# A decoder layer on one core: products with the values on 17 columns instead of 68, and the first pair of k projected ahead of q

## The reference

```python
x = x + mamba(layernorm(x))                            # state-space block, chunks of 64 tokens
x = x + cross_attention(layernorm(x), ctx, mask)       # 16 heads of 64
x = x + ffn(layernorm(x))                              # self attention, then experts

# cross_attention: q from x, k and v from the context
scores = q @ k.T + mask ; ctx = softmax(scores) @ v ; return ctx @ Wo.T

# self attention inside ffn: 16 query heads of 16, 4 key heads, causal, rotary
k = repeat(k, 4) ; v = repeat(v, 4)
scores = where(causal, q @ k.T / 4, -inf) ; out = softmax(scores) @ v ; return out @ wo

# experts: top 2 of 4, gated
```

## Time and profile before

| | us |
|---|---|
| median of 3 runs | 1392.12 |
| lowest and highest run | 1389.46, 1392.37 |
| the profiled execution | 1387.37 |
| its span, first to last instruction | 1385.5 |
| TensorE busy | 1252.3 |
| VectorE busy | 941.3 |
| ScalarE busy | 677.8 |
| GpSimd busy | 271.7 |

### The profile page before, as it was taken

The page is one execution under the profiler, slowest core; times in us unless marked ns, Lnnn a source line. Parts: engine busy times, 40 slices in busy tenths (PEclk is TensorE's granted clock), DMA queues, the critical chain, the costliest instruction groups (busy, mean ns, idle before and its releaser), DMA issues. The chain is left out here.

```text
span 1385.5 us, 25269 instructions
## 1 busy us (share of the span) xinstructions
PE 1252.3 (90%) x8404; PEld 1108.9 (80%) x8404; DVE 941.3 (68%) x2935; ACT 677.8 (49%) x1527; POOL 271.7 (20%) x281
## 2 busy tenths in 40 slices
PE   5889998999899898998998989899897479999997
PEld 4668988867799797778988967799797458888886
DVE  6867767777576676756767776577676875555553
ACT  4737627653565474635636654466374413333332
POOL 2001005110000330100005110000250084333332
PEclk9999999999999999999999999999999579999999
DMA  6026400010452001016500010453611012222221
GB/s 250 1 47 144 115 17 1 1 61 1 116 138 53 16 1 62 1 29 152 126 16 1 1 61 1 106 125 75 229 61 34 1 23 39 38 35 38 39 40 23
DMA packets 45661, 80.38 MB, mean 58 GB/s; under 512 B 8448, under 2 KB 18176, under 8 KB 45024
## 3 DMA queue, kind: packets, MB, share of 16 engines
q1 hardware_dynamic: 37376, 69.19, 18.5%
q0 software_dynamic: 6720, 9.18, 4.1%
q10 hardware_dynamic: 1440, 0.39, 0.1%
HBM read 28.01 MB, written 8.78 MB: 27 GB/s over the span
## 5 line engine op out<-in xcount | busy, mean ns | idle before, releaser
L1036 ACT ACTIVATE b_pp<-b_pp,b_nm 128x256 f32<-128x256 f32 x256 | 116.0, 501 | 83.6 <-DVE b_nm L1074 82.7
L912 PEld LDWEIGHTS bank<-b_va,b_pt 128*128 128x128 f32 x1024 | 128.6, 193 | 4.4
L912 PE MATMUL bank<-b_va,b_pt 128*128 128x65 f32 x1024 | 129.2, 270 | 0.0
L1371 PE MATMUL bank<-c_v,c_pt 128*128 128x68 f32 x768 | 102.2, 269 | 4.1 <-DVE c_pt L1597 3.5
L1371 PEld LDWEIGHTS bank<-c_v,c_pt 128*128 128x128 f32 x768 | 97.2, 191 | 7.8 <-DVE c_pt L1597 7.0
L1074 DVE CUSTOM_DVE_ANT_0 b_pp<-bank,mask 128x256 f32<-128x256 f32 x256 | 97.0, 417 | 0.0
L100 PE MATMUL bank<-e_up_low,e_xh 128*128 x210 | 90.8, 432 | 6.6 <-DVE e_xl L208 5.0
L1899 ACT ACTIVATE e_th<-bank 128x512 f32<-128x512 f32 x35 | 21.0, 601 | 152.8 <-PE bank L102 152.8
L1349 PE MATMUL bank<-c_kv,c_qv 128*128 128x128 f32 (+1 forms) x512 | 89.2, 298 | 0.0
L197 PE MATMUL bank<-identr 128*128 128x512 f32 x274 | 75.6, 426 | 14.9 <-DVE a_cv L617 8.2
L1589 DVE CUSTOM_DVE_ANT_0 c_pp<-bank,const 128x128 f32<-128x128 f32 (+1 forms) x256 | 80.0, 350 | 11.3 <-PE bank L1349 10.8
(11 more groups left out here) (403 smaller groups left out, 3658.2 us busy)
## 6 DMA issues: line engine op xcount, KB each, us to landing
b_kst<-b_kh SPq DMA_DIRECT2D x128, 128.0 KB, 2.3
k_low_twice<-b_kl SPq DMA_DIRECT2D x128, 128.0 KB, 2.4
b_qst<-b_ql SPq DMA_DIRECT2D x64, 128.0 KB, 2.4
raw_up<-in_w SPq DMA_DIRECT2D x4, 768.0 KB, 10.4
raw_down<-in_w SPq DMA_DIRECT2D x4, 768.0 KB, 12.1
XN<-in_x SPq DMA_DIRECT2D x5, 512.0 KB, 3.8
context<-in_ctxT SPq DMA_DIRECT2D x4, 512.0 KB, 5.9
mask<-in_mask SPq DMA_DIRECT2D x4, 512.0 KB, 6.8
```

The costliest lines, as they stand in the source:

```text
L912: ins = pe.matmul(O2[u % 2][:, at:at + VW], pt[:, n % 2, kt * S + qt * P:kt * S + (qt + 1) * P], va[:, b * QT + kt, 2 * j + hp, :], start= ...
L1036: act.activation(pp[:, n % 3, qt, :], pp[:, n % 3, qt, :], ACT.Exp, bias=nm[:, n % 4, qt:qt + 1], scale=-1.0).then_inc(s["probs_exp"], 1)
L1371: ins = pe.matmul(OB[u % 2][:, at:at + AKV * AVW], pt[:, n % 4, i * P:(i + 1) * P], v[:, b * QT + kt].rearrange("p a b -> p (a b)"), start ...
```

## The change

Two edits, independent of each other. In cross attention TensorE's list starts with k0 and v4 and then q0, v5, where it started with v4, v5, q0, k0; ScalarE and VectorE take the results in the new order, and `projected`, which gives the count that ScalarE waits for, is changed to fit. SP's list is the same. In self attention `values` multiplies with the 17 columns of its head's own key head, and `normalise` reads them where they now lie.

```diff
         def projected(j, which):
-            return 2 * j + which + 1 if j < 2 else 2 * j + (1 - which) + 1
+            return 2 * j + which + 1 if j == 1 else 2 * j + (1 - which) + 1
...
             ins.then_inc(s["x_turned"], 1)
+            project(0, 1)
             project_v(4)
-            project_v(5)
             pe.wait_ge(s["x_low"], KD)
             project(0, 0)
-            project(0, 1)
+            project_v(5)
             project_v(6)
             project_v(7)
...
                 part_high(act, uh[:, k, :], T2[k][:]).then_inc(s["x_high"], 1)
+            place(0, 1)
             place_v(1)
             place_v(2)
+            place(0, 0)
             place_v(3)
             place_v(4)
-            place(0, 0)
-            place(0, 1)
             place_v(6)
...
                 part_low(dve, ul[:, k, :], T2[k][:], uh[:, k, :]).then_inc(s["x_low"], 1)
+            place_low(0, 1)
+            place_low(0, 0)
             place_v(5)
-            place_low(0, 0)
-            place_low(0, 1)
             place_v(7)
...
             def values(n):
                 u, hp = n // 2, n % 2
-                b = where(n)[1]
+                m, b, _ = where(n)
...
                 for qt, i, kt in ((0, 0, 0), (1, 1, 0), (1, 2, 1)):
-                    at = (hp * QT + qt) * AKV * AVW
-                    ins = pe.matmul(OB[u % 2][:, at:at + AKV * AVW], pt[:, n % 4, i * P:(i + 1) * P],
-                                    v[:, b * QT + kt].rearrange("p a b -> p (a b)"), start=kt == 0, stop=kt == qt)
+                    at = (hp * QT + qt) * AVW
+                    ins = pe.matmul(OB[u % 2][:, at:at + AVW], pt[:, n % 4, i * P:(i + 1) * P],
+                                    v[:, b * QT + kt, m], start=kt == 0, stop=kt == qt)
...
-                src = OB[u % 2][:, 0:2 * QT * AKV * AVW].rearrange("p (h q d) -> p h q d", h=2, q=QT)
+                src = OB[u % 2][:, 0:2 * QT * AVW].rearrange("p (h q d) -> p h q d", h=2, q=QT)
                 o = rc[:, u % 2].rearrange("p (h q) -> p h q", h=2)
-                ch.link(dve.reciprocal(o, src[:, :, :, m * AVW + AD]))
+                ch.link(dve.reciprocal(o, src[:, :, :, AD]))
...
-                                  src[:, :, :, m * AVW:m * AVW + AD],
+                                  src[:, :, :, 0:AD],
```

## The result

The kernel became slower. The median of four runs is 1436.16 us (1427.26 to 1481.56), beside 1391.12 us for the kernel before (four runs, 1389.46 to 1392.37). The ratio is 1.0313, with an interval of 1.027 to 1.0357; it leaves out the run of 1481.56 us, in which the clock was lowest. The profiled execution took 1427.49 us, its span is 1425.6 us, 40.1 us more than before.

The account below looks back on a forecast made before the run. Cross attention was taken as bound by TensorE, busy 102.98 of 108.10 us, with waits at its start to win. Part one 4 x 2.2 + 2 x 0.15 = 9.1 us, part two 0: from 1392.12 to 1383.0 us, range 1376.5 to 1388.5.

Parts of the forecast that it names:

- Part one, k's first pair first: Start of cross attention: k0 in v4's place removes the 1.8 us wait for q; 9.1 us won over four groups.
- Where the stall goes next: Cross attention: ScalarE's copy of k2 waits 1.7 us for k1's transfers, leaving a shift of 2.2 us a group.
- The clock at this place: Cross-attention start: granted clock falls behind the gaps in two groups, as now; between 2.6 us won and 2.6 lost.
- Part two, 0 for the columns: Self attention: 17 columns for 68 win 0 us, since weight loads about 0.11 us apart set the pace.
- the rival of 18 us: Self attention: TensorE streams fewer columns and they pay, 18 us more won, 1365 us; chance 0.04.
- the estimate of 4.5 us from the Trainium skill's spacing rule: Self-attention products: (30.8 - 25) ns x 768 = 4.5 us won, making the sum 13.6; placed with the 0.04 rival.
- the last rival: Self-attention head-loop pauses: clock falls, 1.3 us each, seven eat the 9.1, ten make it slower; chance 0.11, 0.07 slower.

Follow-up runs that it names:

- the order alone: The changed kernel with `values` and `normalise` as before (68 columns), only the new cross-attention order kept: 1380.35 us, ratio 0.9938 to the kernel before.
- The experiment with k1 early: New order with 68 columns, and k1 and q1 moved ahead of v6 and v7 so k1 is sent earlier: 1371.05 us, ratio 0.986.
- the columns alone: The kernel before with only the 17 columns in self attention, old order kept: four runs of 1437.45, 1463.92, 1497.40 and 1505.48 us.

## Why the prediction was wrong

**Part one, k's first pair first: right, in place and in size.** The sum said 9.1 us; the cross stages lost 8.6, and the order alone won 8.7 us.
- The steps of group 0 came within 0.4 us, and the whole stage began 0.43 us earlier than in the kernel before (GpSimd's setting of the ones at 86.53, before at 86.96), so against the stage's start they came within 0.1: SP's first k transfer at 89.70 (said 90.05), the second issue for q begins by 95.4 (said 95.8), the first scores at 100.05 (100.5), the first masking at 100.72 (101.1). The wait for q is gone.
- "Where the stall goes next" was right: the copy of k2 waits, at 104.48 (104.1), for 2.38 us in group 0 and 1.55 in the others, where 1.7 was said. Against the stage's start that is 0.8 us late in group 0, where one of k1's transfers took 3.1 us to land and not 2.3, and to 0.1 us as said in group 1. In group 3 the second transposes come 2.1 us earlier, measured from the setting of the ones (2.2 said). The experiment with k1 early showed that it is k1's transfers that hold the copy.
- "The clock at this place": two falls of 1.3 us were taken. Before, groups 1 and 2 fell; after, group 0 alone falls, and it takes 3.4 us longer than groups 1 to 3, of which 0.8 are the longer wait for k1's transfers. Without these the stages lost 437.23 - 2.6 - (428.60 - 3.4) = 9.4 us, so the 9.1 holds. That the two falls taken and the one that came cost about the same is luck.

**Part two, 0 for the columns: right at full clock, wrong as an account of what the edit does.** Loads 0.112 us apart with 17 columns, and 1366.59 us beside 1366.06, show that fewer columns win nothing that can be told from the spread; the rival of 18 us and the estimate of 4.5 us from the Trainium skill's spacing rule did not come. But the argument asked only what the columns cost at the clock of the rows. The streamed columns also kept that clock up, at a pause that is in the loop either way.

**Two steps failed, both about the clock in self attention.** The first is the 0 of part two, which took the clock as given ("stages of the same length, clock 1.00"): in the profiled execution the 17 columns cost 51.0 us, in two stages. The second is the price in the last rival, which was there for this case: "Each fall costs 1.3 us, as in group 1". The rival named the right place, the pause of the earlier trace rows, and the right direction; at 1.3 us it took ten falls to be slower. A fall costs 25.8 us, and one is enough, against the 9.1 won. The 1.3 us was read where the products behind the fall are four transposes, six products of 512 columns and eight of 65, and the clock comes back within the stretch of the earlier trace rows. That this would also hold in a loop with 17 columns was never argued; the price was carried over from one kind of work to another. The runs show the difference directly: the loop with 68 columns raised the clock some 6 us after the work began again, in three stages of four, and lost about 3.9 us; the loop with 17 did not raise it in the 53 us that were left of it, and ten wide products raised it.

The chance of 0.11 rested on "the pauses in this loop are short, and no self-attention stage falls now". The clock of 1.00 in the earlier trace rows was read as a property of the pause. It was one of the pause and of the columns around it: pauses of 0.77 to 0.92 us let the clock go in two stages of four with 17 columns, and those of 0.76 to 0.98 us in none with 68.

**What stays open.** In the profiled execution groups 0 and 2 kept their clock at the same pause at which groups 1 and 3 lost it, and in the columns alone groups 2 and 3 fell. The length of the pause does not decide it: groups 0 to 3 waited 0.90, 0.84, 0.77 and 0.92 us in the kernel after, and 0.90, 0.82, 0.76 and 0.91 in the columns alone; and the pause of 1.19 us at the start of the loop lost no clock. No run here tells what does. Nor is it shown what the chip counts; the runs tell only that at 17 columns the clock falls at this pause and stays down to the end of the loop, that at 34 one run of five took as long as two falls would make it, and that at 68 none fell at the short pause.

## What to carry to other kernels

An edit that makes TensorE stream less per weight load can be free in time and still cost the clock: look at every pause in the loop, not only the longest (here 0.84 us lost the clock, and 1.19 us at the start did not), and ask what would raise the clock again behind it. The price of a fall is to be read from work like that which follows it, for it is the time until the clock comes back, and a loop that does not raise it pays to its end. When a start-up stall is removed, follow the serial queue to the next buffer that comes free late; here that gave a second win as large as the first, in part because a fall of the clock behind the stall went with it.

## What was unexpected in the hardware

- TensorE busy in 40.00 of 40.00 us, by the profile, with the granted clock at 0.50 throughout. Being busy without a gap, as the profile counts it, did not raise it.
- A pause of 0.84 us was enough to lose the clock in a loop that had held 1.00 until then, through a pause of 1.19 us too.
- At the low level weight loads follow each other almost twice as slowly, here (527.26 - 525.98)/6 = 0.213 us, against 0.112 at full clock, and with them the whole step: 2.77 us with 17 columns and with 68. The timeline of weight loads in the kernel after, group 1:

```profile
525.98 1.40 PEld L1371 LDWEIGHTS bank<-c_v,c_pt 128*128 128x128 f32 x6
527.26 0.97 PEld L1349 LDWEIGHTS bank<-c_kv,c_qv 128*128 128x128 f32 x4
```
